# Ternary feed-forward behind attention: the apply ahead of the row chain in weight preparation, and a feed-forward loop six groups deep

## The chip, the cores and the metric

The kernel runs on all 8 cores of one Trainium2 chip (two dies of four cores). Every core runs the same program on its own share of the tokens; nothing is exchanged between them. The metric is the device time of the slowest core in microseconds.

## The reference

One layer of attention and one feed-forward layer, each between two layer norms:

```python
x = x + layernorm(attn(layernorm(x), Wq, Wk, Wv, Wo))
x = x + layernorm(ffn(layernorm(x), fast_b, w_fc, w_proj, u, v, gate))

def bitlinear(x, w_latent):              # the weights become -1, 0 or 1
    scale = clip(mean(abs(w_latent), axis=1, keepdims=True), 1e-05, None)
    tern = clip(round(w_latent / scale), -1.0, 1.0)
    return x @ (tern * scale).T
def ffn(x, ...):
    h = bitlinear(x, w_fc) + gate * (x @ v.T @ fast_b.T @ u.T)
    r = maximum(h, 0.0)
    return bitlinear(r * r, w_proj)
```

x is (2, 16384, 1024) in float32, w_fc is 4096 x 1024, w_proj 1024 x 4096. Attention (16 heads of 64) sees 4 sink tokens and the last 512 tokens, so under the causal mask only the last 516 tokens of each sequence get anything from it; 129 of them fall to each core.

## The kernel before, in words

The program is written as one list of operations for each engine. The class `Em` collects them (`E.op`, `E.wait`, `E.gwait` for a buffer's guards, `E.gset` to set one), and `replay` issues them, so all instructions of the profile have line 114. Each engine works through its own list strictly in the order in which it was written; a wait holds everything behind it on that engine. The tiles' names tell the places apart.

**Start.** The norm of the 516 context tokens and of the 129 active ones.

**Preparation with attention between.** There are 64 units of preparation, 32 of kind fc (`w_fc`, 128 hidden columns each) and then 32 of kind pj (`w_proj`), and 32 pieces of attention: 8 for K, 8 for Q, 16 for the heads. The program writes one piece of attention, then two steps of preparation, and so on: K pieces and then Q pieces stand between pairs of fc units, heads between pairs of pj units. A unit (generator `mk_prep`, from line 666) has these parts:

- A1: SP loads 512 KB into one of the two halves of `stg` (unit number modulo 2). Twice, for the positive and the negative part: ACT writes a relu of it to `sgn1`, DVE the remainder to `lnscr` (called `plo`), and TensorE sums both over partitions with a column of ones.
- A2a, the row chain: DVE reduces the sums (`srowp`, two reduces), adds, scales and takes the reciprocal.
- A2b: (fc) ACT squares; TensorE broadcasts the row over partitions; ACT copies it into `hsc2` or `osch` and into `rbb`.
- A3, the apply: DVE multiplies `stg` by `rbb` (for fc also `u2T`), compares with -0.5 into `sgn1` and writes the ternary values to `Sfc` or `Spj`. This frees the half of `stg`: the load of the unit after next waits for it. It is the fourth part of a unit and is run one step late, in the step of the next unit.

`prep_step` (line 827) takes the next unit through A1, A2a and A2b and runs the A3 of the unit before in between. 1 MB loads of `wbuf` (the attention weights, on POOL's queue) happen when half of a weight matrix has been used, that is ahead of K 0 and 4, Q 0 and 4, heads 0 and 8.

**After that** come the low-rank term (added into `Sfc`), the output projection and its norm.

**The feed-forward loop**, 16 tiles of 256 tokens. Hidden units go in 32 groups (`hc`) of 128. `emit_fc(j, hc)`: 8 matmuls into `pb0` or `pb1` in turn; for even groups ACT, for odd ones DVE takes the scaled relu into `rpp`, and DVE multiplies it with the sums into `r2s`, of which there are five. `emit_proj(j, hc)`: 8 matmuls from `r2s` that accumulate into banks `pb2` to `pb5`. A tile writes fc group `hc` and the projection of group `hc` - 5 by turns. At a tile's end come the last five projections, then the first four fc groups of the next tile (`fc_head`), the evacuation of the projection banks by ACT and DVE into `fsq` and `stg` (here `fscr`), fc group 4, the sums of norm LN2 (TensorE over `fsq`), eight matmuls of `zrow` that clear the projection banks, and the next turns. The rest of LN2, the store, the load of the next `xtl` and the norm LN1 of the next tile are laid into the turns at fixed numbers `hc` (7 to 29).

Of the kernel before, what the change touches and what calls it, by code (L numbers as in the profile page):

```python
# [8 lines left out]
BF16 = mybir.dt.bfloat16  # L9
# [16 lines left out]
TT = 256  # L26
NTILE = TOK // TT
DCN = D // 128
HCN = HF // 128
# [89 lines left out]
def build_nc(n_tiles=NTILE):  # L119
# [24 lines left out]
    E = Em()  # L144
# [4 lines left out]
    with ExitStack() as octx:  # L149
# [181 lines left out]
        with ExitStack() as actx:  # L331
# [495 lines left out]
            def prep_step():  # L827
                nonlocal pi
                if pi >= len(prep_units):
                    return  # L830
                kind, idx = prep_units[pi]
                g = mk_prep(kind, idx)
                next(g)
                next(g)
                if prev_g[0] is not None:
                    adv(prev_g[0])
                next(g)
                prev_g[0] = g
                pi += 1
# [86 lines left out]
        with ExitStack() as bctx:  # L926
# [3 lines left out]
            fsq = bsb("fsq", [128, DCN * 512], BF16)  # L930
            fscr = stg
            E.gset("fscr", "sV")
            r2s = [bsb(f"r2s{i}", [128, TT], BF16) for i in range(5)]
            rpp = [bsb(f"rpp{i}", [128, TT], F32) for i in range(2)]

            xn3_t = [v3(x, TT) for x in xn_t]
# [57 lines left out]
            def emit_fc(j, hc):  # L994
# [10 lines left out]
                if hc % 2 == 0:  # L1005
                    E.gwait("scalar", f"rpp{hc % 2}")
                    E.wait("scalar", "sP", cF)
                    if j == 0 and hc == 0:
                        E.wait("scalar", "sA", hsc_ready[-1])
                    E.op("scalar", "activation", rpp[hc % 2][:],  # L1010
                         bank[:, 0:TT], AF.Relu,
                         scale=hsc2[:, hc:hc + 1], inc="sA")
                    cR = E.cnt["sA"]
                    E.gwait("vector", f"r2s{hc % 5}")
                    E.wait("vector", "sP", cF)
                    E.wait("vector", "sA", cR)
                else:
                    E.gwait("vector", f"rpp{hc % 2}")
                    E.wait("vector", "sP", cF)
                    E.op("vector", "tensor_scalar", rpp[hc % 2][:],  # L1020
                         bank[:, 0:TT], hsc2[:, hc:hc + 1], 0.0,
                         ALU.mult, ALU.max)
                    E.drain("vector")
                    E.gwait("vector", f"r2s{hc % 5}")
                E.op("vector", "tensor_tensor", r2s[hc % 5][:],
                     bank[:, 0:TT], rpp[hc % 2][:], ALU.mult, inc="sV")
                r2_of[j][hc] = E.cnt["sV"]
                E.gset(key, "sV")
# [2 lines left out]
            def emit_proj(j, hc):  # L1031
                E.wait("tensor", "sV", r2_of[j][hc])
                for oc in range(OCN):
                    bank = pbk[2 + oc // 2]
                    E.op("tensor", "matmul",
                         bank[:, (oc % 2) * TT:(oc % 2) * TT + TT],
                         s_pj[:, hc * D + oc * 128:hc * D + oc * 128 + 128],
                         r2s[hc % 5][:], start=False,
                         stop=(hc == HCN - 1 and oc % 2 == 1),
                         inc=("sP" if oc == OCN - 1 else None))  # L1040
                E.gset(f"r2s{hc % 5}", "sP")

            def fc_head(j):
                r2_of[j] = [0] * HCN
# [31 lines left out]
            ln1 = None  # L1076
            for j in range(n_tiles):
                emit_fc(j, 4)
                if pend2 is not None:
                    adv(pend2)  # L1080
                for bnk in range(4):
                    E.gwait("tensor", f"pbproj{bnk}")
                    if j == 0 and bnk == 0:
# [4 lines left out]
                    E.op("tensor", "matmul", pbk[2 + bnk][:, 256:512],  # L1088
                         zrow[0:1, 0:128], zrow[0:1, 0:256],
                         start=False, stop=False)  # L1090
                for hc in range(5, HCN):
                    emit_proj(j, hc - 5)
                    emit_fc(j, hc)
                    if pend2 is not None:
                        if hc == 7:
# [25 lines left out]
                            E.gset("fscr", "sV")  # L1121
                            tile_state[j + 1] = ln1[1][0]
                E.gset(f"xn{j % 2}", "sP")
                for hc in range(HCN - 5, HCN):
                    emit_proj(j, hc)
                c_proj = E.cnt["sP"]
                if j + 1 < n_tiles:
# [154 lines left out]
```

How the kernel before makes its waits and increments, by code:

```python
    def replay(self, eng_name, engobj, sems):  # L106
        for act in self.q[eng_name]:
            if act[0] == "w":
                engobj.wait_ge(sems[act[1]], act[2])
            elif act[0] == "d":
                engobj.drain()
            else:
                _, fname, args, kwargs, incv = act
                inst = getattr(engobj, fname)(*args, **kwargs)
                if incv is not None:
                    inst.then_inc(sems[incv[0]], incv[1])
```

## Time and profile before

| | us |
|---|---|
| time, median of 2 runs | 2964.59 (2952.68 to 2976.49) |
| the profiled execution | 2966.91 |
| its span on the slowest core (core 1) | 2965.4 |
| spans of the eight cores | 2891.6 to 2965.4 |
| TensorE matmul, busy | 1708.8 (58%) |
| DVE busy | 1317.6 (44%) |
| ACT busy | 485.7 (16%) |
| load of `stg`, issue to landing (median of 64) | 3.6 |

All rows are from core 1 unless another is named. A time in a timeline or chain is the start in us from the beginning of the span, the next number how long the instruction (or the run of xN instructions) took. What stands in brackets is how long the engine was idle before and what ended the wait. PEclk is the granted TensorE clock as a share of 2.4 GHz. The chain of work goes back from the end of a stretch, at each step to what released the instruction.

### The profile page before, as it was taken

What the parts mean: (1) busy time and instruction counts of PE and PEld (TensorE: products, weight loads), DVE (VectorE), ACT (ScalarE), POOL (GpSimd) and SP (SyncE); (2) the same over time, 40 slices, a digit from 0 to 9 for tenths busy, and PEclk for the clock granted to TensorE, in tenths of its full rate; (3) what the DMA queues carried; (4) which work ended last, traced back from release to release, by engine and by line L of the source; (5) the groups of instructions that cost most, each with busy time, mean ns of one, the idle gap of its engine ahead of it and who ended that gap; (6) DMA issues with size and microseconds to landing.
All of it is one profiled execution on the core that took longest, in us unless ns stands there. A gap on an engine that the chain in (4) does not pass through costs nothing.

```text
span 2965.4 us, 32026 instructions; the slowest of 8 cores (2891.6 to 2965.4 us)
## 1 busy us (share of the span) xinstructions
PE 1708.8 (58%) x10888; PEld 1113.3 (38%) x10888; DVE 1317.6 (44%) x2281; ACT 485.7 (16%) x1089; POOL 20.8 (1%) x36
## 2 busy tenths in 40 slices
PE   2433332222333333333668888878787887888876
PEld 0111110001111111111156666666565665656655
DVE  1244444344444544544634444444444444444434
ACT  1111111111111111121011111111111111111111
POOL 0000000000000000000000000000000000000000
PEclk7555555555555555555578888898888888888888
DMA  2001010101000100001000000010111101111010
GB/s 44 25 22 43 28 43 29 43 29 43 21 29 22 43 22 29 22 29 36 14 29 1 29 29 29 29 30 1 29 29 29 29 1 29 29 29 30 1 29 29
DMA packets 49201, 80.53 MB, mean 27 GB/s; under 512 B 12019, under 2 KB 37748, under 8 KB 48004
## 3 DMA queue, kind: packets, MB, share of 16 engines
q1 hardware_dynamic: 28244, 44.60, 5.1%
q0 software_dynamic: 4160, 17.11, 2.4%
q10 hardware_dynamic: 16640, 16.78, 2.2%
q8 instruction: 93, 1.52, 0.2%
q14 instruction: 64, 0.52, 0.1%
HBM read 70.42 MB, written 16.78 MB: 29 GB/s over the span
## 4 chain that ended last, share of the span: by engine, by line
PE 46%; DVE 27%; DMA 12%; issue 7%; ACT 6%; DVEq 1%; ACTq 0%; SPq 0%; POOLq 0%
PE pb L114 46%; DVE lnscr L114 6%; DMA xtl<-xT 5%; DVE srowp L114 4%; DMA stg<-wfc_st 4%; DVE stg L114 4%; DVE srow L114 4%; ACT sgn L114 2%; DVE Sfc L114 2%; DMA stg<-wpj_st 2%; DMA ctxXg<-ctxT 1%; ACT srow L114 1%; ACT lnscr L114 1%; DVE r2s L114 1%; DVE sgn L114 1%
## 5 line engine op out<-in xcount | busy, mean ns | idle before, releaser
L114 PE MATMUL pb<-xn,Sfc 128*128 128x256 bf16 x4096 | 591.8, 294 | 120.8 <-DVE r2s L114 115.1
L114 PE MATMUL pb<-r2s,Spj 128*128 128x256 bf16 x4096 | 587.1, 295 | 0.0
L114 PEld LDWEIGHTS pb<-xn,Sfc 128*128 128x128 bf16 x4096 | 423.9, 105 | 220.6 <-issue 142.9
L114 PEld LDWEIGHTS pb<-r2s,Spj 128*128 128x128 bf16 x4096 | 427.1, 106 | 103.6 <-issue 27.3
L114 PE MATMUL pb<-sgn,cvecb 128*1 128x512 bf16 x256 | 129.2, 608 | 521.1 <-DVE lnscr L114 521.1
L114 DVE TENSOR_TENSOR r2s<-pb,rpp 128x256 bf16<-128x256 f32 x512 | 215.7, 423 | 425.4 <-ACT rpp L114 370.1
L114 DVE SCALAR_TENSOR_TENSOR lnscr<-stg,sgn 128x1024 bf16<-128x1024 f32 x128 | 156.8, 1225 | 463.6 <-ACT sgn L114 309.7
L114 ACT ACTIVATE rpp<-pb,hsc 128x256 f32<-128x256 f32 x256 | 122.3, 478 | 993.5 <-PE pb L114 970.8
L114 PE MATMUL pb<-lnscr,cvecb 128*1 128x512 bf16 x472 | 206.7, 567 | 72.0 <-ACT lnscr L114 71.2
L114 PEld LDWEIGHTS pb<-sgn,cvecb 128*1 128x1 bf16 x256 | 14.5, 80 | 585.8 <-issue 585.8
L114 DVE TENSOR_SCALAR rpp<-pb,hsc 128x256 f32<-128x256 f32 x256 | 122.7, 479 | 232.9 <-PE pb L114 230.1
L114 ACT ACTIVATE sgn<-stg 128x1024 bf16<-128x1024 f32 x128 | 128.0, 1048 | 232.5 <-DMA stg<-wfc_st 139.7
L114 PE MATMUL pb<-srowp,crows 1*128 1x128 f32 (+1 forms) x128 | 43.7, 437 | 199.8 <-ACT srowp L114 118.4
L114 DVE TENSOR_REDUCE srowp<-pb 1x128 f32<-1x512 f32 (+1 forms) x128 | 81.7, 674 | 136.3 <-PE pb L114 136.3
L114 PEld LDWEIGHTS pb<-srowp,crows 1*128 1x128 f32 x128 | 31.8, 307 | 257.4 <-issue 257.4
L114 PEld LDWEIGHTS pb<-lnscr,cvecb 128*1 128x1 bf16 x472 | 51.9, 114 | 186.6 <-issue 175.4
L114 PE MATMUL pb<-srow,crows 1*128 1x256 f32 (+3 forms) x172 | 58.4, 473 | 93.7 <-DVE srow L114 93.7
L114 PE MATMUL pb<-fsq,cvecb 128*1 128x512 bf16 x128 | 56.4, 620 | 64.1 <-DVE fsq L114 59.3
L114 PE MATMUL pt<-identb,lnscr 1*128 1x1 bf16 (+3 forms) x160 | 17.4, 232 | 113.6 <-DVE lnscr L114 113.6
L114 PEld LDWEIGHTS pb<-srow,crows 1*128 1x128 f32 x172 | 36.0, 244 | 116.4 <-issue 112.6
L114 DVE TENSOR_TENSOR stg<-stg,pb 128x2048 f32<-128x2048 f32 x32 | 72.9, 2278 | 2.4 <-PE pb L114 2.3
L114 DVE TENSOR_TENSOR stg<-stg,rbb 128x1024 f32<-128x1024 f32 x64 | 73.6, 1150 | 0.0
(104 smaller groups left out, 1270.2 us busy)
## 6 DMA issues: line engine op xcount, KB each, us to landing
stg<-wfc_st SPq DMA_DIRECT2D x32, 512.0 KB, 3.6
stg<-wpj_st SPq DMA_DIRECT2D x32, 512.0 KB, 3.6
outT<-stg ACTq DMA_DIRECT2D x16, 1024.0 KB, 9.3
xtl<-xT SPq DMA_DIRECT2D x16, 512.0 KB, 7.1
xtl<-xT POOLq DMA_DIRECT2D x16, 512.0 KB, 9.5
ctxXg<-ctxT SPq DMA_DIRECT2D x8, 256.0 KB, 2.9
wbuf<-wk POOLq DMA_DIRECT2D x2, 1024.0 KB, 12.1
wbuf<-wq POOLq DMA_DIRECT2D x2, 1024.0 KB, 9.3
```

The source lines that it names most:

```text
L114: inst = getattr(engobj, fname)(*args, **kwargs)
```

## The change

Two independent edits. In `prep_step` the apply (A3) of the unit before is written between A1 and A2a of the current one, and no longer between A2a and A2b. In the feed-forward loop `r2s` gets a sixth buffer, fc group 5 is written right behind group 4, and the projection trails the fc groups by six.

```diff
                 g = mk_prep(kind, idx)
                 next(g)
-                next(g)
                 if prev_g[0] is not None:
                     adv(prev_g[0])
+                next(g)
                 next(g)
                 prev_g[0] = g
...
-            r2s = [bsb(f"r2s{i}", [128, TT], BF16) for i in range(5)]
+            r2s = [bsb(f"r2s{i}", [128, TT], BF16) for i in range(6)]
...
             for j in range(n_tiles):
                 emit_fc(j, 4)
+                emit_fc(j, 5)
                 if pend2 is not None:
                     adv(pend2)
...
-                for hc in range(5, HCN):
-                    emit_proj(j, hc - 5)
+                for hc in range(6, HCN):
+                    emit_proj(j, hc - 6)
                     emit_fc(j, hc)
...
                 E.gset(f"xn{j % 2}", "sP")
-                for hc in range(HCN - 5, HCN):
+                for hc in range(HCN - 6, HCN):
                     emit_proj(j, hc)
```

Every `hc % 5` that picks an `r2s` buffer becomes `hc % 6`. On DVE this is the third unit of preparation before the change; `lnscr` is A1, `srowp` A2a, and the four rows from `stg` to `Sfc` are the A3 of the second unit:

```order
L114 SCALAR_TENSOR_TENSOR lnscr<-stg,sgn 128x1024 x2
L114 TENSOR_REDUCE srowp<-pb 1x128 x2
L114 TENSOR_TENSOR srowp<-srowp 1x128
L114 TENSOR_SCALAR srowp<-srowp 1x128
L114 RECIPROCAL srowp<-srowp 1x128
L114 TENSOR_TENSOR stg<-stg,rbb 128x1024
L114 TENSOR_TENSOR u2T<-u2T,rbb 16x128
L114 TENSOR_SCALAR sgn<-stg 128x1024
L114 SCALAR_TENSOR_TENSOR Sfc<-stg,sgn 128x8x128
```

And after it, at the same place:

```order
L114 SCALAR_TENSOR_TENSOR lnscr<-stg,sgn 128x1024 x2
L114 TENSOR_TENSOR stg<-stg,rbb 128x1024
L114 TENSOR_TENSOR u2T<-u2T,rbb 16x128
L114 TENSOR_SCALAR sgn<-stg 128x1024
L114 SCALAR_TENSOR_TENSOR Sfc<-stg,sgn 128x8x128
L114 TENSOR_REDUCE srowp<-pb 1x128 x2
L114 TENSOR_TENSOR srowp<-srowp 1x128
L114 TENSOR_SCALAR srowp<-srowp 1x128
L114 RECIPROCAL srowp<-srowp 1x128
```

The four rows of the apply have moved ahead of the four of the row chain; nothing else differs, and the same holds for all 63 units that have one before them. On TensorE this is the border between the first two tiles before the change (`xn,Sfc` are fc groups of 8 matmuls, `r2s,Spj` projections, `fsq` the sums of LN2):

```order
L114 MATMUL pb<-xn,Sfc 128x256 x8
L114 MATMUL pb<-r2s,Spj 128x256 x40
L114 MATMUL pb<-xn,Sfc 128x256 x40
L114 MATMUL pb<-fsq,cvecb 1x512 x8
L114 MATMUL pb<-zrow 128x256 x8
L114 MATMUL pb<-r2s,Spj 128x256 x8
L114 MATMUL pb<-xn,Sfc 128x256 x8
```

And after it:

```order
L114 MATMUL pb<-xn,Sfc 128x256 x8
L114 MATMUL pb<-r2s,Spj 128x256 x48
L114 MATMUL pb<-xn,Sfc 128x256 x48
L114 MATMUL pb<-fsq,cvecb 1x512 x8
L114 MATMUL pb<-zrow 128x256 x8
L114 MATMUL pb<-r2s,Spj 128x256 x8
L114 MATMUL pb<-xn,Sfc 128x256 x8
```

One projection (8 matmuls) now stands at the end of the tile, and one fc group ahead of the sums and no longer behind them.

## Rows read from the trace of the kernel before

**Rows 1.** Stages: stretch, length, busy us of PE, PEld, DVE, ACT, POOL; PEclk, DMA.

```profile
143.00:730.00 587.00, 176.12 (x525) 58.84 (x525) 260.32 (x344) 91.20 (x181) 2.12 (x4) 0.51 0.13 34
1512.00:2960.00 1448.00, 1198.13 (x8692) 915.96 (x8692) 644.64 (x1225) 245.36 (x540) 10.47 (x14) 0.85 0.08 22
```

**Rows 2.** Waits from 143 to 1410 us: total us, times, longest.

```profile
DVE lnscr L114 <- ACT sgn L114: 309.7, 64, 10.5
...
ACT sgn L114 <- DMA stg<-wfc_st: 139.7, 30, 10.1
...
ACT sgn L114 <- DMA stg<-wpj_st: 92.8, 16, 6.4
```

**Rows 3.** Chain of one fc step, 620 to 641 us: start, us, what.

```profile
626.87 1.24 DVE lnscr L114
...
630.21 1.29 DVE srowp L114 x2
...
633.17 1.15 DVE stg L114
...
636.78 3.71 DMA stg<-wfc_st
...
640.57 1.06 ACT sgn L114
```

**Rows 4.** ACT's timeline, a step with a Q unit behind it.

```profile
653.26 0.27 ACT L114 ACTIVATE rbb<-pb 128x128 f32<-128x128 f32 x1
654.12 0.28 ACT L114 ACTIVATE Qt<-pb 128x129 bf16<-128x129 f32 x1 [0.58 <-PE pb L114]
659.01 2.00 ACT L114 ACTIVATE sgn<-stg 128x1024 bf16<-128x1024 f32 x2 [4.61 <-DMA stg<-wfc_st]
```

**Rows 5.** ACT's timeline, a step with a K unit behind it.

```profile
319.36 0.66 ACT L114 ACTIVATE Kt<-pb 128x512 bf16<-128x512 f32 x2 [3.32 <-PE pb L114]
321.56 2.00 ACT L114 ACTIVATE sgn<-stg 128x1024 bf16<-128x1024 f32 x2 [1.54 <-DMA stg<-wfc_st]
```

**Rows 6.** Timeline behind the last Q unit, where `wbuf` is loaded anew.

```profile
690.85 0.28 ACT L114 ACTIVATE Qt<-pb 128x129 bf16<-128x129 f32 x1 [0.58 <-PE pb L114]
691.29 0.53 POOL L114 DMA_DIRECT2D wbuf<-wv  x1 [152.73 <-PE pb L114]
...
701.22 2.00 ACT L114 ACTIVATE sgn<-stg 128x1024 bf16<-128x1024 f32 x2 [10.10 <-DMA stg<-wfc_st]
```

**Rows 7.** Timeline of a pj step, and the first `sgn` behind the next head.

```profile
1004.66 1.28 DVE L114 TENSOR_REDUCE srowp<-pb 1x32 f32<-1x512 f32 x2 [2.12 <-PE pb L114]
...
1006.87 1.15 DVE L114 TENSOR_TENSOR stg<-stg,rbb 128x1024 f32<-128x1024 f32 x1
...
1007.91 0.17 ACT L114 ACTIVATE rbb<-pb 128x32 f32<-128x32 f32 x1
...
1008.99 1.22 DVE L114 SCALAR_TENSOR_TENSOR Spj<-stg,sgn 128x1024 bf16<-128x1024 f32 x1
...
1013.84 2.00 ACT L114 ACTIVATE sgn<-stg 128x1024 bf16<-128x1024 f32 x2 [5.75 <-DMA stg<-wpj_st]
...
1039.28 1.99 ACT L114 ACTIVATE sgn<-stg 128x1024 bf16<-128x1024 f32 x2
```

**Rows 8.** TensorE's timeline at the border of a tile.

```profile
2229.58 3.57 PE L114 MATMUL pb<-fsq,cvecb 128*1 128x512 bf16 x8 [3.95 <-DVE fsq L114]
2233.08 1.88 PE L114 MATMUL pb<-zrow 1*128 1x256 bf16 x8
2234.90 1.89 PE L114 MATMUL pb<-r2s,Spj 128*128 128x256 bf16 x8
2236.58 1.91 PE L114 MATMUL pb<-xn,Sfc 128*128 128x256 bf16 x8
```

**Rows 9.** TensorE's timeline in the middle of a tile, groups at the full clock.

```profile
2266.83 1.04 PE L114 MATMUL pb<-r2s,Spj 128*128 128x256 bf16 x8
2267.70 1.04 PE L114 MATMUL pb<-xn,Sfc 128*128 128x256 bf16 x8
```

**Rows 10.** The ten us from the sums of LN2 on, as in rows 1.

```profile
2229.00:2239.00 10.00, 9.42 (x38) 4.87 (x39) 1.17 (x4) 0.00 (x0) 0.00 (x0) 0.52 0.01 2
```

**Rows 11.** The feed-forward loop on core 6, as in rows 1.

```profile
1498.00:2888.00 1390.00, 1155.02 (x8692) 894.68 (x8692) 644.58 (x1224) 244.91 (x540) 10.47 (x14) 0.89 0.07 23
```

More of the change, by code:

```diff
@@ L1013, in emit_fc @@
                     cR = E.cnt["sA"]
-                    E.gwait("vector", f"r2s{hc % 5}")
+                    E.gwait("vector", f"r2s{hc % 6}")
                     E.wait("vector", "sP", cF)
@@ L1023, in emit_fc @@
                     E.drain("vector")
-                    E.gwait("vector", f"r2s{hc % 5}")
-                E.op("vector", "tensor_tensor", r2s[hc % 5][:],
+                    E.gwait("vector", f"r2s{hc % 6}")
+                E.op("vector", "tensor_tensor", r2s[hc % 6][:],
                      bank[:, 0:TT], rpp[hc % 2][:], ALU.mult, inc="sV")
@@ L1037, in emit_proj @@
                          s_pj[:, hc * D + oc * 128:hc * D + oc * 128 + 128],
-                         r2s[hc % 5][:], start=False,
+                         r2s[hc % 6][:], start=False,
                          stop=(hc == HCN - 1 and oc % 2 == 1),
                          inc=("sP" if oc == OCN - 1 else None))
-                E.gset(f"r2s{hc % 5}", "sP")
+                E.gset(f"r2s{hc % 6}", "sP")
             def fc_head(j):
```

## The prediction

> **What bounds the kernel now.** I read first the stages [rows 1]: the stretch in which the weights are turned into ternary values ("prep"), with attention laid between, runs from 143 to about 1410 us, and the feed-forward loop over 16 tiles from 1512 to 2960. In prep no engine is near full: DVE is busy 260 of 587 us, TensorE 176 and at the lower of its two levels (granted 0.51, that is 1.2 GHz). So the stretch is a chain of waits, and what counts is which wait ends last. The waits of that stretch [rows 2] name it: DVE waits 309.7 us in 64 waits for ACT's first `sgn`, and ACT in front of it waits 139.7 + 92.8 = 232.5 us for the DMA that loads `stg`. The chain of one ordinary step [rows 3] shows why that load is late: a load may only start when the apply part of the unit two before has ended, since there are two halves of `stg`; the apply stands behind the row chain of the current unit. Second `lnscr` ends at 628.11, the reduce starts at 630.21 after an idle 2.1 us (it waits for TensorE), the apply starts at 633.17, the load goes out at 636.78, and the next `sgn` starts at 640.57. The feed-forward loop is bound by TensorE with a few holes in each tile; the one that the change touches is at the border of two tiles, where it waits for DVE's `fsq`.
>
> **Change 1, the order inside a prep step.** No instruction is added or removed. DVE's apply of the former unit moves ahead of the reduce of the current one. The step has 64 instances (32 of kind fc, 32 of kind pj), and the time from a step's second `lnscr` to the next step's first `sgn` is what changes; from `sgn` to second `lnscr` nothing moves. The terms, by what lies between two steps:
>
> - *fc, the second of a pair (nothing between).* The apply starts at 628.11 instead of 633.17, 5.0 us earlier, and its load lands 5.0 us earlier. The reduce cannot start before the apply is done. The apply is 3.6 us long (633.17 to the load's issue at 636.78), 2.1 of which fall into the idle time in front of the reduce, so the reduce and all behind it (row chain, ACT's square, TensorE's broadcast, ACT's copy into `rbb`) come 1.55 us later. What is late next is that copy: in the step of [rows 4] it ended at 653.53, and will end 1.55 later; `sgn` can follow at 655.1 instead of 659.0. Gain 3.9 us. There are 15 of these (unit 1 is loaded with no wait as it is), 58.5 us.
> - *fc with a Q unit between.* ACT's `Qt` copy stands in front of `sgn` and ended at 654.40 [rows 4]; 1.55 later it ends at 655.95, so `sgn` starts at 656.0 instead of 659.0. Gain 3.0 us, six times, 18 us.
> - *The two Q steps after which `wbuf` is loaded anew.* In [rows 6] the `wbuf` load goes out at 691.29, just ahead of the `stg` load, and `sgn` starts at 701.22, 10.1 us after ACT became free: both transfers share the time. After the change the `stg` load is out 5 us earlier and lands before the `wbuf` load, which waits for the end of Q's matmuls (and these come 1.55 later). ACT is free at 691.13, so `sgn` starts at 691.13 + 1.55 + 0.05 = 692.7 instead of 701.2. Gain 8.5 us, twice, 17 us.
> - *fc with a K unit between.* ACT's `Kt` ended at 320.02 and `sgn` started at 321.56 [rows 5]; 1.55 later `Kt` ends at 321.57. The load is early now, but ACT is not. Nothing gained or lost, seven times.
> - *pj, the second of a pair.* In [rows 7] the reduce starts at 1004.66 after 2.12 us idle, the apply runs from 1006.87 to 1010.21 (3.35 us), `rbb` is copied by 1008.08, `sgn` starts at 1013.84. After the change the apply starts 4.3 us earlier (1004.66 - 2.12 = 1002.54), the reduce 1.35 later, `rbb` ends at 1009.4 and the load lands at about 1009.6. Gain 4.2 us, 16 times, 67 us.
> - *pj with an attention head between.* Here the load was hidden by the head: `sgn` at 1039.28 follows ACT's last copy of the head, and the head's own matmuls stand behind this step's broadcast on TensorE. All of it comes 1.35 us later, and the apply that used to run beside it is now in front. Loss 1.35 us, 15 times, and 1.55 once behind the last fc unit: 21.8 us.
>
> Sum: 58.5 + 18 + 17 + 67 - 21.8 = 139 us. The cover that hides the apply now is the 2.1 us in which DVE waited for TensorE's sums; without it each step would pay the whole 3.35 to 3.6 us, which is 2.1 x 63 = 132 us, and the gain would be gone. Nothing but the `stg` load on SP's queue waits for the apply. Bounds of this term: the loads could be somewhat longer in their new place or ACT's copy a little later, so a quarter of a microsecond on each of the 39 gaining steps, 10 us either way, and 10 us more if `wbuf` and `stg` still meet.
>
> The Trainium skill says under "Key Constraints" of "Trainium Kernel Development and Optimization" that transfers from SP's, ACT's and POOL's queues run on the same 16 DMA engines and interleave. By that rule the `wbuf` load will stretch some other transfer once it no longer meets this one; the trace agrees that the two stretch each other. The sum would be the same less at most one such stretch for each of the two.
>
> **Change 2, the feed-forward loop one group deeper.** `r2s` has six buffers instead of five; fc group 5 moves ahead of the LN2 sums and the projection trails by six groups instead of five. A pass has the same matmuls. On TensorE the border of a tile is now six projection groups, six fc groups (0 to 5), sums, zero rows. What is hidden: fc 5 needs bank 1, free since DVE's r2s of group 3, which comes before the evacuation on DVE's queue, so it runs at once inside the 3.95 us in which TensorE waited for `fsq` [rows 8]. What waits on DVE and ACT is not longer: their share of group 5 is queued behind `fsq`. Every later wait of the tile (for the rows of the two norms, for the next `xtl`) is tied to an fc group's number on both sides and moves along; the sixth projection group comes back at the end of the tile. So a tile is shorter by one group of eight matmuls, which takes 0.87 us at the full clock [rows 9], for 15 borders 13 us. In the rows of the border that same group stands in the slow stretch behind the sums and takes 1.7 us, so 26 us if all of it is won. The slow stretch [rows 10] has a granted clock of 0.52, the lower level (1.2 GHz), over 10 us. Core 6 runs the same loop in 1390 us at 0.89 where the slowest core takes 1448 at 0.85 [rows 11, 1]; so by the clock alone this loop can be 58 us shorter, or, for a core like 6, longer. I take 13 us, the price at the full clock, since the hole in front of the slow stretch stays a hole: what runs at half rate in that stretch is then another group, and what is saved is saved later. The ends are 0 (a new wait eats it) and 70 us (13 and the 58 between cores).
>
> **The rivals.**
>
> *A: the clock comes back.* A shorter hole at the border might spare the slow stretch. The 10 us at half rate would shrink by 4 to 5 us a tile, 15 x 4.6 = 69 us: 2967 - 139 - 69 = 2759. For it: that a core with a higher granted clock exists [rows 11]. Against: the hole only shrinks from 3.95 to about 3.0 us, and the eight sums and eight zero rows behind it are the same. The Trainium skill ("TensorE: Matmul & The Clock Gate", section "HAM oscillation — how this bites in real kernels") states that a wait for data in every pass of a loop throws the clock back to half rate every time, and that keeping the engine fed avoids it. By that rule this could go either way here, depending on whether the shorter hole still counts as one; the trace agrees with it as far as the slow stretch stands right behind the hole.
>
> *B: the loads get no shorter path.* If a load in its new place were stretched as in the step with `wbuf`, where `sgn` came 10.1 us after ACT was free and not 4.6 [rows 6, 4], 5.5 us would be lost against the 5.0 (pj: 4.3) by which it goes out earlier: fc and Q steps lose 0.5 us, pj pairs 1.2, heads 1.35: 2967 + 23 x 0.5 + 16 x 1.2 + 22 - 13 = 3007, within 2%. Against: only the steps next to a `wbuf` load show it; the others run beside the same traffic as before.
>
> *C: slower.* The place is the reduce in each of the 63 steps. If the load was not what `sgn` waits for, every step would pay the 1.35 to 1.55 us by which the reduce moves, 31 x 1.55 + 32 x 1.35 = 91 us: 2967 + 91 - 13 = 3045. It decides from the point at which ACT waits less than 1.5 us for the load per step. Against it stands the 232.5 us in 46 waits [rows 2], 5 us each; for it only that the K steps, with 1.5 us of wait, are just at that point.
>
> **How the numbers follow.** The profiled execution took 2966.9 us with a span of 2965.4. 2966.9 - 139 - 13 = 2815. The median of the runs is 2964.6, 2.3 us less, so I forecast 2813. The two runs shown are 24 us apart, so nothing under 2% (59 us) can be told from no change. Chances: the forecast (2780 to 2850) 0.80, rival A with all it gives (below 2780) 0.13, B 0.04, C 0.03. Faster by over 2%: 0.93; within 2%: 0.04; slower: 0.03. The range 2768 to 2850 takes in 13 us and a little more of missed gain in each change upwards, and the larger part of A downwards.
>
> **What would show it.** Right, if ACT's wait for `stg` falls from 232.5 us to almost nothing in the stretch of [rows 2]; if DVE no longer waits before the reduce; if from one first `sgn` to the next an fc pair's second step takes 14.5 us (659.01 - 640.57 = 18.4 before [rows 3, 4]) and a Q step 15.4, if a pj pair's second step is 4.2 us shorter, K steps the same and head steps 1.35 longer; if the feed-forward loop starts 139 us earlier; and if the wait for `fsq` is 3.0 us with the tile 0.9 us shorter. Wrong, if ACT still waits 3 us or more for the load, if something other than `rbb`, `Qt` or the head's copy stands in front of `sgn`, or if the tile loop's time moves by more than 30 us, which would be the clock and not the group.

## The result and the profile after

The changed kernel takes 2735.88 us (median of 11 runs) where the kernel before, with more runs, now stands at 2973.29 us (10 runs). The ratio is 0.920, with a 95% interval of 0.916 to 0.923: 8% faster, 237 us. The forecast was 2813 us with a range of 2768 to 2850, so the direction held and the size did not: 152 us were forecast, 139 for change 1 and 13 for change 2, and 237 came. In some executions the cores of one die run longer at a lower granted clock, and the ratios leave those out.

The profiled execution took 2720.68 us with a span of 2718.1 on its slowest core (now core 5); against the profiled execution before that is 246 us. The prediction was summed against that one, in two terms, and both can be read apart. From a core's first to its last `sgn`, the preparation took 1240.6 to 1257.6 us on the eight cores before and takes 1093.0 to 1097.5 us now: mean 1248.9 and 1096.2, 153 us less, where 139 had been forecast (155 on the slowest cores). From a core's first fc group to its end, the loop took 1393.6 to 1452.8 us before and takes 1348.8 to 1359.0 now: 74 us less in the mean and 94 on the slowest core, where 13 had been forecast.

The page of the changed kernel, its busy times, its clock by fortieths of the span, and the groups for TensorE's two large kinds of matmul, for ACT's `sgn` and for DVE's reduce:

```profile
PE 1642.5 (60%) x10888; PEld 1083.5 (40%) x10888; DVE 1314.0 (48%) x2281; ACT 482.5 (18%) x1089; POOL 20.8 (1%) x36
...
PEclk8555555555555555555599889899989988898988
...
L114 PE MATMUL pb<-xn,Sfc 128*128 128x256 bf16 x4096 | 566.3, 285 | 107.4 <-DVE r2s L114 101.1
L114 PE MATMUL pb<-r2s,Spj 128*128 128x256 bf16 x4096 | 561.0, 287 | 0.0
...
L114 ACT ACTIVATE sgn<-stg 128x1024 bf16<-128x1024 f32 x128 | 128.0, 1051 | 5.4 <-DMA stg<-wpj_st 5.0
...
L114 DVE TENSOR_REDUCE srowp<-pb 1x128 f32<-1x512 f32 (+1 forms) x128 | 81.3, 670 | 2.1 <-PE pb L114 2.1
```

ACT's wait in front of `sgn`, 232.5 us for the load of `stg` in [rows 2], is 5.4 us. DVE's wait in front of the reduce, 2.1 us in every step of [rows 3] and [rows 7], is 2.1 us in all 64 together. That is change 1 as it was meant. DVE and ACT are as busy as before (1314.0 and 482.5 us against 1317.6 and 485.7), but TensorE, which has the same 10888 matmuls, is busy 66 us less (1708.8 before).

The stages of the changed kernel, to be held against [rows 1] (columns as there), and the loop's waits of TensorE (total us, times, longest):

```profile
143.00:650.00 507.00, 186.26 (x608) 64.38 (x607) 271.78 (x366) 93.81 (x197) 2.12 (x4) 0.52 0.15 41
...
1385.00:2700.00 1315.00, 1105.39 (x8484) 864.53 (x8481) 625.22 (x1195) 240.84 (x531) 10.48 (x14) 0.91 0.07 24
```

```profile
PE pb L114 <- DVE r2s L114: 101.1, 65, 6.7
...
PE pb L114 <- DVE srow L114: 63.9, 31, 3.7
PE pb L114 <- DVE fsq L114: 43.1, 15, 2.9
```

The granted clock of the preparation is 0.52 against 0.51 (the lower level, 1.2 GHz, nearly throughout). In the loop it rose from 0.85 to 0.91. In the kernel before the same three waits, counted from the first fc group on, were 115.1, 63.1 and 59.3 us. So of the 94 us on the slowest core, 30 are shorter waits: 16 in front of the LN2 sums, which is where the forecast had 13, and 14 for `r2s`, mostly behind the load of `xtl`. The norms' rows are waited for as before. The 14 us are a matter of the core more than of the change: before, four cores waited 113 to 115 us for `r2s` and four 95 to 99, and now all eight wait 100 to 108, 2 us less in the mean. The rest, some 64 us on the slowest core and 57 of the 74 in the mean of the cores, is not waiting at all. It is time in which TensorE is busy with the same number of matmuls: the two large kinds together were busy 591.8 + 587.1 = 1178.9 us before and 566.3 + 561.0 = 1127.3 now, 52 us less. (One kind's start overlaps the other's end, so these sums count some time twice; without that they are 1042 and 1000.)

A part of that is chance. Beside 0.5 and 1 the traces have a third value of the granted clock, 0.81. Here are 26 us of it on core 1 of the kernel before (columns as in [rows 1]):

```profile
1524.80:1550.80 26.00, 26.00 (x200) 21.55 (x199) 8.29 (x19) 3.69 (x8) 0.00 (x0) 0.81 0.00 1
```

Core 1 had 77 us of it in the loop, cores 0, 2 and 3 had 72 to 85, cores 4 to 7 none, and in the profile of the changed kernel no core had any. At 0.81 instead of 1 the 77 us cost an estimated 14 us (77 x 0.19) of the slowest core's 94. Cores 4 to 7 alone gained 71 us in the mean, so the 74 stand.

What the change moved is the time at the lower level. Of the loop it was 371 us before and is 236 us now, in the mean of the cores. Around the 15 borders (from 4 us before the sums start to 9 behind it) it fell from 138 to 62 us, around the broadcast of LN2's rows (from 3 us before its start to 6 behind) from 45 to 7, and elsewhere by some 20.

The border of a tile on TensorE in the changed kernel:

```profile
1943.91 2.11 PE L114 MATMUL pb<-xn,Sfc 128*128 128x256 bf16 x16 [0.26 <-DVE r2s L114]
1948.90 1.89 PE L114 MATMUL pb<-fsq,cvecb 128*1 128x512 bf16 x8 [2.88 <-DVE fsq L114]
1950.72 1.04 PE L114 MATMUL pb<-zrow 1*128 1x256 bf16 x8
1951.69 1.05 PE L114 MATMUL pb<-r2s,Spj 128*128 128x256 bf16 x8
1952.58 1.04 PE L114 MATMUL pb<-xn,Sfc 128*128 128x256 bf16 x8
```

The sixteen `xn,Sfc` matmuls are fc groups 4 and 5, one behind the other, and the hole behind them is 2.88 us and not 3.95. The eight sums behind it then take 1.89 us and not 3.57, the zero rows 1.04 and not 1.88, the first projection 1.05 and not 1.89 [rows 8]: all of them at the upper level (2.4 GHz), where they ran at the lower one. It is not so at every border. This is the next one:

```profile
2031.34 2.79 PE L114 MATMUL pb<-fsq,cvecb 128*1 128x512 bf16 x8 [2.87 <-DVE fsq L114]
2034.05 1.89 PE L114 MATMUL pb<-zrow 1*128 1x256 bf16 x8
```

With the same hole the clock fell while the sums ran. Over the 15 borders of all eight cores, the sums ran wholly at the upper level at 41 of 120; in the kernel before, with a hole of 3.95 us, at none.

### The profile page after: what moved, and what is told of

Same layout as the page of the kernel before. It is cut to its first block, busy times and chain, and to the rows that moved or that the text cites. A ratio compares the mean times of both kernels' runs of the same rounds, so it can differ in the third digit from the quotient of the medians.

```text
span 2718.1 us, 32025 instructions; the slowest of 8 cores (2700.0 to 2718.1 us)
## 1 busy us (share of the span) xinstructions
PE 1642.5 (60%) x10888; PEld 1083.5 (40%) x10888; DVE 1314.0 (48%) x2281; ACT 482.5 (18%) x1089; POOL 20.8 (1%) x36
## 4 chain that ended last, share of the span: by engine, by line
PE 45%; DVE 27%; issue 12%; DMA 9%; ACT 7%; DVEq 1%; ACTq 0%; SPq 0%; POOLq 0%
PE pb L114 44%; DVE stg L114 6%; DMA xtl<-xT 5%; DVE srowp L114 4%; DVE srow L114 4%; DVE lnscr L114 4%; ACT sgn L114 2%; DMA stg<-wpj_st 2%; DVE sgn L114 2%; DMA ctxXg<-ctxT 2%; ACT srow L114 1%; DVE r2s L114 1%; ACT lnscr L114 1%; DVE fsq L114 1%; DVE nmb L114 1%
## 5 line engine op out<-in xcount | busy, mean ns | idle before, releaser
L114 PE MATMUL pb<-xn,Sfc 128*128 128x256 bf16 x4096 | 566.3, 285 | 107.4 <-DVE r2s L114 101.1
L114 PE MATMUL pb<-r2s,Spj 128*128 128x256 bf16 x4096 | 561.0, 287 | 0.0
L114 PEld LDWEIGHTS pb<-xn,Sfc 128*128 128x128 bf16 x4096 | 410.7, 102 | 199.3 <-issue 134.4
L114 PEld LDWEIGHTS pb<-r2s,Spj 128*128 128x128 bf16 x4096 | 416.2, 103 | 90.0 <-issue 25.2
L114 DVE SCALAR_TENSOR_TENSOR lnscr<-stg,sgn 128x1024 bf16<-128x1024 f32 x128 | 156.8, 1225 | 390.0 <-ACT sgn L114 236.3
L114 DVE TENSOR_SCALAR srow<-pb 1x256 f32<-1x256 f32 (+3 forms) x86 | 27.4, 354 | 103.2 <-PE pb L114 103.0
L114 DVE TENSOR_TENSOR srow<-srow 1x256 f32<-1x256 f32 (+3 forms) x129 | 46.9, 364 | 58.4 <-ACT srow L114 49.5
```

The costliest lines, as they stand in the source:

```text
L114: inst = getattr(engobj, fname)(*args, **kwargs)
```

## The experiments

There were twelve runs in four sets, each set on a chip of its own: e1 to e4, e5 to e8, e9 to e11, e12. Each set had runs of the kernel before on its chip (medians 2956, 2957, 2953 and 2960 us), and the ratios are against these. "Loop" is the time from a core's first fc group to its end in the profiled execution, as the mean of the eight cores and on the one with the longest; before: 1428 and 1453 us. "Half rate" is the part of it at the lower level, mean of the cores. In the texts of the expectations T1 is the theory that the two changes are separate and that holes cost TensorE their length and then the clock behind them; T2 to T8 are its rivals.

| kernel | median us | ratio, 95% interval | loop, mean / longest | wait for `fsq`, 15 borders | granted clock 1620 to 2420 us, cores | half rate |
|---|---|---|---|---|---|---|
| before | 2956 | 1 | 1428 / 1453 | 59.3 | 0.85 to 0.89 | 371 |
| after (first chip) | 2736 | 0.920 (0.916 to 0.923) | 1354 / 1359 | 43.1 | 0.91 to 0.93 | 236 |
| e1_apply_only | 2818 | 0.954 (0.944 to 0.965) | 1420 / 1456 | 59.2 | 0.83 to 0.90 | 352 |
| e2_deep_only | 2899 | 0.985 (0.977 to 0.992) | 1369 / 1387 | 43.1 | 0.89 to 0.92 | 252 |
| e3_fill8 | 2923 | 0.992 (0.987 to 0.998) | 1380 / 1405 | 45.9 | 0.87 to 0.91 | 264 |
| e4_deep_late | 2925 | 0.993 (0.989 to 0.998) | 1390 / 1408 | 59.4 | 0.87 to 0.89 | 329 |
| e5_after_again | 2748 | 0.928 (0.920 to 0.935) | 1371 / 1379 | 43 | 0.87 to 0.92 | 259 |
| e6_deep_again | 2901 | 0.980 (0.970 to 0.989) | 1373 / 1395 | 43 | 0.89 to 0.92 | 268 |
| e7_fill20 | 2706 | 0.915 (0.908 to 0.921) | 1333 / 1357 | 10.4 | 0.92 to 0.94 | 186 |
| e8_sums_late | 2699 | 0.912 (0.906 to 0.918) | 1323 / 1331 | none | 0.92 to 0.93 | 220 |
| e10_ln1_late | 2629 (2585 to 2717) | none | 1220 / 1225 | none | 0.95 to 0.96 | 134 |
| e9_schedule | 2536 | 0.859 (0.852 to 0.867) | 1166 / 1168 | none | 0.97 to 0.98 | 80 |
| e11_before_fill28 | 2852 | 0.965 (0.956 to 0.974) | 1341 / 1350 | 13.4 | 0.92 to 0.94 | 186 |
| e12_bcast28 | 2520 | 0.852 (0.842 to 0.861) | 1150 / 1159 | none | 0.97 to 0.98 | 64 |

### e1: change 1 alone

```diff
                 g = mk_prep(kind, idx)
                 next(g)
-                next(g)
                 if prev_g[0] is not None:
                     adv(prev_g[0])
+                next(g)
                 next(g)
```

> Change 1 alone (the apply ahead of the row chain), the feed-forward loop as before. Theory T1 (the two changes are separate: change 1 shortens the preparation by some 155 us, change 2 shortens the loop by some 95, most of it by TensorE's clock): about 2973 - 155 = 2818 us, the preparation as in the changed kernel (first to last sgn about 1095 us), the loop from its first fc group to the end about 1450 us on the slowest core as before. Rival T2 (the loop is quicker because it starts from another moment or because the preparation changed the state of the clock or of the cores against each other): clearly under 2790 us, with a loop near 1360 us.

Measured 0.954, 135 us at the kernel before's 2956; the preparation is 1095.8 us in the mean, as in the changed kernel, and the loop 1420 us, as before (1428). That is T1: change 1 does nothing for the loop. The expected 2818 us was met by luck, since the kernel before is 17 us faster on this chip than on the first. The 135 us agree with the preparation's 153 within the interval (104 to 165 us), but the slowest core of this profile, core 2, was also granted 0.81 for 244 us of its loop, an estimated 46 us (244 x 0.19). Theory T1 takes no account of that level. In the loop it shows on two cores each of e1, e2, e3 and e5, and on none of e4 and e6 to e12. DVE's timeline of one of its fc steps shows where the forecast of the preparation was too low:

```profile
291.47 1.23 DVE L114 SCALAR_TENSOR_TENSOR lnscr<-stg,sgn 128x1024 bf16<-128x1024 f32 x1 [2.40 <-PE pb L114]
292.62 1.22 DVE L114 TENSOR_TENSOR stg<-stg,rbb 128x1024 f32<-128x1024 f32 x1
...
295.00 1.23 DVE L114 SCALAR_TENSOR_TENSOR Sfc<-stg,sgn 128x1024 bf16<-128x1024 f32 x1
296.14 1.27 DVE L114 TENSOR_REDUCE srowp<-pb 1x128 f32<-1x512 f32 x2
```

The apply starts at 292.62 although the second `lnscr` runs until 292.70, and the reduce at 296.14 although the apply runs until 296.23. Neither waits for anything, so the next instruction starts some 0.1 us before the one ahead has ended. The reduce starts 296.14 - 292.70 = 3.44 us behind the second `lnscr`; before it was 2.11. That is a delay of 1.33 us and not the 1.55 of the forecast. The same happens on ACT, in a step with a K unit:

```profile
304.29 0.66 ACT L114 ACTIVATE Kt<-pb 128x512 bf16<-128x512 f32 x2 [3.32 <-PE pb L114]
304.83 2.00 ACT L114 ACTIVATE sgn<-stg 128x1024 bf16<-128x1024 f32 x2
```

`sgn` starts 0.12 us before `Kt` ends (304.95), while the forecast had it 0.05 behind. Together these are 0.22 + 0.17 = 0.39 us.

### e2: change 2 alone

All of the change but the hunk in `prep_step`.

> Change 2 alone (six r2s buffers, fc group 5 ahead of the LN2 sums), the preparation as before. T1: about 2973 - 90 = 2880 us (2870 to 2895), the wait for fsq 2.9 us, a granted clock of about 0.91 in the loop. T2: about 2960 us (13 us gained, as forecast), clock 0.85.

Measured 0.985: 2899 us and a loop of 1369 in the mean, 59 us shorter than before. Hole 2.9 us, clock 0.89 to 0.92. The expected 2880 was too low, the 2960 of T2 was too high; the loop and the clock are those of T1. Of the 59 us, 12 are shorter waits of TensorE and 47 busy time.

### e3: eight idle matmuls in the hole

```diff
+            def fill(j, n):
+                E.gwait("tensor", "pt")
+                for k in range(n):
+                    E.op("tensor", "matmul", ptf[:, 0:TT],
+                         s_fc[:, k * 128:k * 128 + 128],
+                         xn_t[j % 2][:, 0:TT], start=True, stop=True)
...
                 emit_fc(j, 4)
+                if j > 0:
+                    fill(j, 8)
```

> The kernel before with eight extra matmuls per tile border, laid into the hole in which TensorE waits for fsq. They multiply fc weights with xn into the bank pt, which nobody reads in the loop, so no work of the loop is taken away and none is done earlier; output unchanged. If the loop is quicker because the shorter hole keeps the clock up (T1): the hole goes from 3.95 to about 3.1 us, the granted clock in the loop rises from 0.85 to about 0.90, and the time falls by 50 to 80 us, to about 2905. Rival T3 (the gain comes from the deeper pipeline, as the projection trailing by six groups, and the clock only follows): no gain, 2970 to 2985 us.

Measured 0.992, an interval that just excludes 1: 23 us by the ratio, and in the profiled executions a loop 48 us shorter in both readings (mean and longest). The kernel does more work and moves none, and it is faster. That speaks for T1 and against T3, but the time fell by less than T1 had expected; the preparation, which was not touched, reads 9 us longer in this profile, and cores 4 and 5 were granted 0.81 for 126 and 131 us of their loops. The time at the lower level around the borders fell from 138 to 58 us, as far as in the changed kernel (62). One border:

```profile
1956.85 1.04 PE L114 MATMUL pt<-xn,Sfc 128*128 128x256 bf16 x8
1960.97 1.89 PE L114 MATMUL pb<-fsq,cvecb 128*1 128x512 bf16 x8 [3.08 <-DVE fsq L114]
1962.79 1.04 PE L114 MATMUL pb<-zrow 1*128 1x256 bf16 x8
```

### e4: six deep, with the hole as before

```diff
                 emit_fc(j, 4)
-                emit_fc(j, 5)
                 if pend2 is not None:
                     adv(pend2)
...
+                emit_fc(j, 5)
                 for hc in range(6, HCN):
```

(against change 2 alone: group 5 stands behind the sums and the zero rows)

> Change 2 alone with fc group 5 written behind the LN2 sums and the zero rows: six buffers and the projection trailing by six groups as in the changed kernel, but the hole in front of the sums as long as before (3.95 us). T1: as the kernel before, 2960 to 2975 us, clock 0.85. T3: most of the 90 us of change 2, about 2885 us.

Measured 0.993. T1 had expected nothing, T3 the whole; the result is about a third to a half of change 2, with 59.4 us of waiting for `fsq` as before. So the order of the groups has a share of its own, which neither theory names. The loop is 38 us shorter in the mean: 7 us are waits and the rest is busy time, so this share too is the clock. It lies at another place. Around the borders the time at the lower level is much as before (145 us against 138), and around the broadcast of LN2's rows it went from 45 us to none. In the 5 us behind that broadcast the granted clock was 0.70 before, in the mean of all borders and cores, and is 1.00 in e4 (0.96 in the changed kernel). The broadcast before, and in e4:

```profile
2246.72 1.10 PE L114 MATMUL pb<-srow,crows 1*128 1x256 f32 x4 [1.16 <-DVE srow L114]
2247.75 1.05 PE L114 MATMUL pb<-r2s,Spj 128*128 128x256 bf16 x8
2248.64 1.76 PE L114 MATMUL pb<-xn,Sfc 128*128 128x256 bf16 x8
```

```profile
2146.27 1.10 PE L114 MATMUL pb<-srow,crows 1*128 1x256 f32 x4 [1.15 <-DVE srow L114]
2147.30 1.05 PE L114 MATMUL pb<-r2s,Spj 128*128 128x256 bf16 x8
2148.18 1.04 PE L114 MATMUL pb<-xn,Sfc 128*128 128x256 bf16 x8
```

The wait is the same 1.15 us. The broadcast comes 15.9 us behind the start of the sums in the mean, and 16.8 before. Why the clock stays up there was not tested. It is not the new order alone that does it: in e11 below, with the old order and the border's hole filled, it is 0.92.

### e5 and e6: both changes, and change 2 alone, on one chip

The changed kernel, and e2, once more.

> The changed kernel once more, on the same chip as the next three. In the first set the two halves alone gave ratios of 0.954 and 0.985 (product 0.940) where both together had given 0.920. If they add up (T1): ratio to the kernel before as the product of the halves on this chip, so close to 0.94 here, and the loop of this kernel as long as the loop of change 2 alone. If they help each other (T4: the loop is quicker behind the shorter preparation): 0.92, and a loop 15 us or more shorter than with change 2 alone.

> Change 2 alone once more, beside the full change on one chip. Loop on the slowest core 1360 to 1390 us, ratio 0.97 to 0.985. T1: the same loop as the full change within 10 us. T4: 15 us or more longer.

Ratios 0.928 and 0.980, loops 1371 and 1373 us in the mean: the same loop behind either preparation, as T1 has it, and no sign of T4 in the traces. The longest loops, 1379 and 1395, differ by 16 us, about as much as cores differ in one execution. The product of e1 and e6 is 0.935, the changed kernel here 0.928 with an interval up to 0.935. On two chips it gave 0.920 and 0.928, so some of the difference between the halves and the whole in the first set may lie in the chip.

### e7: 20 idle matmuls in what is left of the hole

```diff
                 emit_fc(j, 4)
                 emit_fc(j, 5)
+                if j > 0:
+                    fill(j, 20)
```

> The changed kernel with 20 extra matmuls (2.2 us at the full clock) laid into what is left of the hole in front of the LN2 sums (2.9 us), into a bank that nobody reads; no work of the loop moves. If a still shorter hole keeps the clock up for longer (T1): hole below 1 us, time at half rate per tile from 14.4 to 10 us or less, 20 to 40 us quicker than the changed kernel. If the hole of 2.9 us no longer matters (T5): the same time within 10 us.

2706 against 2748 us of the changed kernel on the same chip, 41 us less, loop 38 us shorter in the mean, granted clock 0.92 to 0.94. The wait is 10.4 us at 15 borders, 0.7 each, and the sums ran at the upper level at all 120. T1; a hole of 2.9 us still mattered, and T5 falls.

### e8: useful work in that hole

```diff
                 emit_fc(j, 5)
-                if pend2 is not None:
-                    adv(pend2)
-                for bnk in range(4):
+                for bnk in (2, 3, 0, 1):
...
                     emit_proj(j, hc - 6)
+                    if hc == 6 and pend2 is not None:
+                        adv(pend2)
```

> The changed kernel with useful work in that hole: the zero rows (banks pb4, pb5 first) and projection 0 stand ahead of the LN2 sums and no longer behind them. The banks are free some 1 to 2 us before fsq is ready. T1: the wait for fsq falls from 2.9 us to below 0.5, two waits below 1.3 us each appear in front of the zero rows, a tile is 1.5 us shorter for the work moved and some 1 to 2 more by the clock: 35 to 55 us quicker than the changed kernel. Rival T6 (the later sums delay LN2's row chain, which then holds TensorE at hc 9): no gain, and a wait for srow longer than 1.2 us.

2699 us, 49 less than the changed kernel beside it. The border now:

```profile
2020.62 0.63 PE L114 MATMUL pb<-zrow 1*128 1x256 bf16 x4 [0.53 <-DVE stg L114]
2021.83 0.59 PE L114 MATMUL pb<-zrow 1*128 1x256 bf16 x4 [0.57 <-ACT stg L114]
...
2023.33 1.89 PE L114 MATMUL pb<-fsq,cvecb 128*1 128x512 bf16 x8
...
2032.59 1.10 PE L114 MATMUL pb<-srow,crows 1*128 1x256 f32 x4 [1.15 <-DVE srow L114]
```

Two waits of 0.5 and 0.6 us stand where one of 2.9 was, the sums wait for nothing, and the wait for LN2's rows is 1.15 us as ever, so T6 falls. Of the 48 us by which the mean loop is shorter than in e5, 33 are waits, so most of this gain is the work that was moved. The clock gave little: the lower level takes 20 us around the borders in place of 72 in e5, but behind the broadcast of LN2's rows the granted clock is 0.75 in place of 0.97. What remains in this kernel are the holes that no part of the change touches: 4.9 us in the mean for the load of `xtl`, 2.8 and 1.2 us for the norms' rows.

### e9 and e10: the other holes

```diff
-                        elif hc == 9:
+                        elif hc == 10:
...
-                        if hc == 18:
+                        if hc == 21:
                             ln1 = ln1_start(j + 1)
-                        elif hc == 23:
+                        elif hc == 24:
                             adv(ln1[0])
-                        elif hc == 26:
+                        elif hc == 25:
                             adv(ln1[0])
```

(e9, on top of e8; e10 has the two edits from 18 to 21 and from 23 to 24 alone)

> The kernel of e8_sums_late with the fixed numbers hc of the norms moved: the casts of LN1 from 18 to 21 (its load lands about five groups after it is issued at 15), its sums from 23 to 24, its rows from 26 to 25 with the broadcast left at 27, the broadcast of LN2 from 9 to 10. That takes away the other holes of a tile: 4.9 us for the load, 2.8 for LN1's row chain, 1.2 for LN2's. T1 (holes cost their length and then the clock behind them): a tile 8 to 11 us shorter than in e8, granted clock in the loop above 0.95, total 2699 - 15 x 9 = 2565 us (2530 to 2600). Rival T7 (the holes move instead: the later norm leaves TensorE waiting for xn at the next tile or for a bank, or the power limit takes the clock to 0.81 as two cores of the first set had it): above 2640 us.

> e8_sums_late with the casts of LN1 at hc 21 and its sums at 24, nothing else. T1: the hole of 4.9 us for the load shrinks below 1.5, half the gain of e9: 2620 to 2650 us. T7: 2690 us or more, with a new wait at the tile border.

e9 takes 2536 us, a ratio of 0.859: 14% faster than the kernel before, and 7% faster than the changed one by their ratios. It lies in T1's range of 2530 to 2600, below its middle of 2565. T7 falls, and no core was granted 0.81. e10's four runs took 2585, 2589, 2670 and 2717 us, and no ratio is given; the two shorter ones are below the 2620 to 2650 of T1. Its profiled execution (2584.64 us) has a loop of 1220 us, 103 less than e8's. The `xtl` hole stood at 14 borders; without it the wait for `r2s` fell from 100.7 to 37.6 us on the slowest cores. The page of e9, clock and groups:

```profile
PEclk9555555555555555555557999999999999999998
...
L114 PE MATMUL pb<-xn,Sfc 128*128 128x256 bf16 x4096 | 537.7, 276 | 54.9 <-DVE r2s L114 48.7
L114 PE MATMUL pb<-r2s,Spj 128*128 128x256 bf16 x4096 | 527.4, 276 | 0.0
```

The same 8192 matmuls are busy 1065.1 us here against 1178.9 before, 114 us less, while their number and shapes are the same. Of the holes in front of the norms' rows one is left in a tile of e9, with its trail:

```profile
1990.82 1.10 PE L114 MATMUL pb<-srow,crows 1*128 1x256 f32 x4 [1.15 <-DVE srow L114]
1991.85 1.33 PE L114 MATMUL pb<-r2s,Spj 128*128 128x256 bf16 x8
1992.97 1.91 PE L114 MATMUL pb<-xn,Sfc 128*128 128x256 bf16 x8
1994.68 1.64 PE L114 MATMUL pb<-r2s,Spj 128*128 128x256 bf16 x8
1996.15 1.04 PE L114 MATMUL pb<-xn,Sfc 128*128 128x256 bf16 x8
```

A wait of 1.15 us and four float32 matmuls of a single row, and the three groups behind run at the lower level for a stretch: 1.33, 1.91 and 1.64 us where 1.04 is usual. The length of the wait alone doesn't decide: in the same tile TensorE waited 1.43 us for `r2s` (until 1970.05), and the groups behind took 1.04 us each.

### e11: the whole hole filled, everything else as before

```diff
                 emit_fc(j, 4)
+                if j > 0:
+                    fill(j, 28)
```

(on the kernel before, with the same `fill`)

> The kernel before with 28 extra matmuls (3.1 us at the full clock) in the hole of 3.95 us, against 8 in e3, which gave a ratio of 0.992 and took the mean loop from 1428 to 1380 us. No work of the loop moves. T1: the loop 10 to 40 us shorter still than with 8, ratio 0.975 to 0.99, time at half rate per tile below 14 us. T5 (a hole of 3 us already does not matter): as e3, ratio 0.99.

Measured 0.965, 103 us by the ratio; loop 1341 us in the mean against 1428, and the 8192 useful matmuls busy 561.7 + 553.7 = 1115.4 us against 1178.9. It is a stronger effect than T1 had expected. The preparation, which was not touched, reads 1235.8 us in this profile against 1248.9, so some 13 us of the difference between the two profiles is not from the edit. The border:

```profile
2003.82 3.22 PE L114 MATMUL pt<-xn,Sfc 128*128 128x256 bf16 x28
2007.94 1.89 PE L114 MATMUL pb<-fsq,cvecb 128*1 128x512 bf16 x8 [0.89 <-DVE fsq L114]
```

The sums ran at the upper level at all 120 borders. The clock alone, with no work moved, can bring more than change 2 did: 28 matmuls per tile whose result nobody reads take 3.2 us each time, in which TensorE had been idle anyway. That change 2's own gain is mostly the clock is shown by its busy time (e2).

### e12: the last hole

```diff
-                        elif hc == 27:
-                            adv(ln1[0])
                         elif hc == 28:
                             adv(ln1[0])
                         elif hc == 29:
+                            adv(ln1[0])
+                        elif hc == 30:
                             adv(ln1[0])
```

> e9_schedule with the last hole in front of a norm's broadcast closed: LN1's broadcast at hc 28 instead of 27 (and its two applies at 29 and 30). In e9 TensorE waited 1.15 us there and ran the next three groups at half rate (some 3.4 us per tile). T1: the hole gone and the half-rate stretch behind it too, 1.2 + 1.7 = 2.9 us a tile, 15 tiles, 43 us: ratio to the kernel before 0.845 against 0.859. Rival T8 (holes this short cost their own length alone): 17 us, ratio 0.853. Rival T7 (the later apply makes TensorE wait for xn): no gain.

2520 us, ratio 0.852 with an interval that overlaps e9's and takes in the 0.845 of T1 as well as the 0.853 of T8. So the traces must tell. The wait at the broadcast is gone and TensorE's wait for `srow` in the loop's window is 7.3 us in all against 25.9. The broadcast and what follows:

```profile
2012.74 1.13 PE L114 MATMUL pb<-srow,crows 1*128 1x256 f32 x4
2013.80 1.05 PE L114 MATMUL pb<-r2s,Spj 128*128 128x256 bf16 x8
2014.68 1.04 PE L114 MATMUL pb<-xn,Sfc 128*128 128x256 bf16 x8
```

The stretch at half rate went with the hole: in the 5 us behind the broadcast of LN1's rows the granted clock is 0.99 in the mean of all tiles and cores, and 0.83 in e9. Of the loop's mean, 16 us shorter, some 9 us are busy time of the two large kinds; the time at the lower level fell from 80 to 64 us. So the total agrees with T8's 17 us and the way it comes about does not. Two things stand against T1's 43 us: the wait for `r2s` grew from 48.7 to 63.3 us on the slowest cores, and around the tile borders the lower level took 38 us in place of 29. T7 falls: nothing new waits for `xn`. This is the fastest kernel of the study, 15% faster than the kernel before.

## Why the prediction was wrong

**Change 1: right in mechanism and place, too small by a tenth.** The load no longer sets the start of a step, and what is late next is ACT's copy or its work from the attention piece, as forecast. The time from one first `sgn` to the next, mean over the steps of a kind, on the slowest core of each profile:

| step | times | before us | after us | forecast change | measured |
|---|---|---|---|---|---|
| fc, second of a pair | 15 | 18.37 | 14.15 | -3.9 | -4.2 |
| fc, Q between (all eight) | 8 | 19.88 | 15.09 | -4.4 | -4.8 |
| fc, K between | 7 | 18.47 | 18.09 | 0 | -0.4 |
| pj, second of a pair | 16 | 17.43 | 13.14 | -4.2 | -4.3 |
| a head between | 16 | 24.67 | 25.79 | +1.35 | +1.1 |

All five are off the same way, by 0.1 to 0.4 us. The step that failed is "the reduce and all behind it come 1.55 us later": it was worked out by adding up durations one behind the other with the pause that a wait leaves, and instructions of one engine with no wait between them overlap by about 0.1 us (e1). The whole term was 153 us instead of 139. The two `wbuf` steps behaved as forecast: they are in the second row and became 8.7 and 8.9 us shorter, forecast 8.5.

**Change 2: the term that failed.** The prediction said of the loop: "I take 13 us, the price at the full clock, since the hole in front of the slow stretch stays a hole". The price of the wait was right: TensorE's wait for `fsq` fell by 16 us in 15 borders, forecast 13. What failed is the step from the hole to the stretch behind it, "what runs at half rate in that stretch is then another group": it took the stretch as fixed. The loop became shorter by 74 us in the mean of the cores and 94 on the slowest, and 57 and 64 us of this are busy time of the same matmuls: the time at the lower level fell from 371 to 236 us. The prediction had named this sign itself, a loop that moves by more than 30 us, "which would be the clock and not the group". Rival A had named this and priced it at 69 us with a chance of 0.13, and its 2759 us would have been the nearer forecast. Against it stood the sentence "the hole only shrinks from 3.95 to about 3.0 us"; e3 shows that this much shrinking is worth something even with idle matmuls, e11 that filling the hole is worth 103 us, and e7 that the remaining 2.9 us still cost some 40. Rival A's mechanism was incomplete too: e4 shows that the deeper order alone keeps the clock up behind LN2's rows (1.00 granted against 0.70), a second place that no part of the prediction looked at.

Here the rule of the Trainium skill ("TensorE: Matmul & The Clock Gate", section "HAM oscillation — how this bites in real kernels") was the better guide: a wait in every pass of a loop throws the clock to half rate in every pass. The traces agree in kind: e9 and e12, with few waits left, have a granted clock of 0.97 to 0.98. They don't agree for every wait: one of 1.43 us in e9 has no slow stretch behind it. In the traces the cost falls off gradually as the hole shrinks (0.85 to 0.89 with 4 us, 0.91 to 0.93 with 2.9, 0.92 to 0.94 with less than 1), since it is a matter of how many borders lose the clock: the sums ran wholly at the upper level at 0, 41 and 120 of 120. And even a hole of 1.15 us has a stretch at half rate behind it in e9, which was gone when e12 closed the hole.

**The range.** Its lower end, 2768, would have been reached by a loop gain of 60 us. The prediction had read from the cores of the kernel before that the loop can differ by 58 us by the clock alone, and put the bound for the change at 70 us. What it missed is that the metric is the slowest core: the cores' loops lay between 1394 and 1453 us, and now all eight lie between 1349 and 1359, so the slowest gained 94 us and core 6 only 37. Nor was the clock the whole of the difference between the cores: core 1 waited 115.1 us for `r2s` and core 6 98.6, so some 17 of the 59 us are waits, and an estimated 14 us are core 1's stretches at 0.81.

**What stays open.** Why the deeper order keeps the clock up behind LN2's rows with the same wait (e4), why filling the border's hole does so too (e11), and why e8 loses that again (0.75), no run shows. By the ratios idle filling alone (0.992) and depth alone (0.993) each give about half of change 2 (0.985 and 0.980 in two sets), so its gain cannot be given to the hole alone. These are small effects beside intervals of half a per cent. When a core is granted 0.81 is open too; it came in some executions and not in others.

## What to carry to other kernels

Price a wait of TensorE twice: its own length, and the matmuls behind it that run at half rate. The second can be the larger: e2 saved 12 us of waits and 47 of busy time. It is seen as a fall of busy time of a group whose count and shape did not change. Before moving work to close such a hole, fill it with matmuls that nobody reads: one edit that moves nothing tells what the hole is worth, and here it was 3.5%. Where one buffer half is refilled only after a step's last reader, write that reader where its engine waits anyway.

## What the runs showed of the hardware

Twenty-eight matmuls of 128 x 256 per tile that compute nothing useful made a kernel faster by 103 us (e11), with TensorE's 8192 useful matmuls busy for 64 us less. The eight cores run the same program, and their loops spread over 59 us before and over 10 after. Between core 1 and core 6 some 17 of the 59 us were waits for `r2s`, and the rest was the same matmuls at a lower granted clock. Two cores of a profile could be granted 0.81 for 72 to 249 us of a loop while others of the same die were not (e1: cores 2 and 3 alone). A wait of 1.15 us in front of four float32 matmuls of one row was followed by half rate in some schedules (e9) and not in others (e4), and one of 1.43 us in front of an fc group was not (e9). On DVE and ACT an instruction that waits for nothing starts about 0.1 us before the one ahead of it has ended (292.62 against 292.70, 304.83 against 304.95), which makes sums of durations a little too long wherever waits are absent.
